# A Perceiver block with two mixtures of experts on one core: the first experts' matmuls with the rows as fixed side and the weights moving in two parts, and the second experts' weights chosen on GpSimd

## What is computed

```
# first experts: each row goes to 2 of 8 experts, F = 512, D = 256; no limit of rows per expert
probs = softmax(flat @ Wg); topp, topi = top_k(probs, 2); topp = topp / (sum(topp) + 1e-08)
for e in range(8):
    h = silu(flat @ W1[e]) * (flat @ W3[e])
    out = out + cw[:, e:e + 1] * (h @ W2[e])
# second experts: 2 of 8, F = 1024, each expert takes at most cap = 512 rows, in order
h = gelu(xg @ W1[e] + b1[e]); out = h @ W2[e] + b2[e]
final = zeros.at[buf].add(out * w)
```

## Time and profile before

| | us |
|---|---|
| median of 3 runs | 1272.7 (1271.81 to 1279.18) |
| profiled execution | 1282.01, its span 1280.2 |
| PE busy | 1119.4, 87% of the span |
| POOL busy | 785.9, 61% |
| DVE busy | 737.9, 58% |
| ACT busy | 603.9, 47% |

### The profile page before, as it was taken

One profiled execution on the slowest core, in us unless ns is written; L12 is line 12 of the kernel. 1 busy time (PEld: TensorE's weight loads), 2 busy tenths in 40 slices (PEclk: granted clock), 3 DMA queues, 4 the chain that ended last, 5 costly groups with the idle time before them and its releaser, 6 DMA issues. The chain is left out here.

```text
span 1280.2 us, 28023 instructions
## 1 busy us (share of the span) xinstructions
PE 1119.4 (87%) x8612; PEld 1031.6 (81%) x8613; DVE 737.9 (58%) x2263; ACT 603.9 (47%) x1404; POOL 785.9 (61%) x815
## 2 busy tenths in 40 slices
PE   4799999999999998898899639999998357998888
PEld 2599999999999997687677429999997236888777
DVE  5566666667666664755565572333332666666663
ACT  1556555565555652433767533444443432444331
POOL 0487778777777784144787505666664056667753
PEclk9899999999999997899999869999999667999989
DMA  3221111212111120692000422232322574543400
GB/s 110 75 69 56 50 53 49 70 51 68 53 49 53 54 77 4 152 364 76 1 0 0 65 77 38 46 49 49 49 45 37 167 211 107 148 116 89 103 5 9
DMA packets 72144, 94.24 MB, mean 74 GB/s; under 512 B 14828, under 2 KB 52160, under 8 KB 72096
## 3 DMA queue, kind: packets, MB, share of 16 engines
q1 hardware_dynamic: 53584, 73.00, 18.0%
q0 software_dynamic: 16032, 20.62, 9.9%
q10 hardware_dynamic: 2480, 0.03, 0.1%
HBM read 73.69 MB, written 22.18 MB: 75 GB/s over the span
## 5 line engine op out<-in xcount | busy, mean ns | idle before, releaser
L428 PE MATMUL xa_ob<-xa_v,xa_pT 128*128 128x65 f32 x1024 | 135.1, 276 | 0.2 <-DVE xa_pT L653 0.2
L495 POOL TENSOR_TENSOR xa_qbd<-qs,xw_c_mask8s 128x512 fp32r<-128x512 f32 x128 | 131.8, 1051 | 2.3 <-ACT xa_pr L583 2.2
L2450 PE MATMUL e_yb<-e_w2s,e_hTs 128*128 128x256 f32 x768 | 106.4, 305 | 29.5 <-DVE e_y L2599 20.5
L1862 POOL DMA_INDIRECT e_x<-rows,source x71 | 71.4, 1006 | 94.0 <-DMA rows<-weight 40.7
L2450 PEld LDWEIGHTS e_yb<-e_w2s,e_hTs 128*128 128x128 f32 x768 | 103.4, 214 | 31.4 <-DVE e_y L2599 21.7
L428 PEld LDWEIGHTS xa_ob<-xa_v,xa_pT 128*128 128x128 f32 x1024 | 126.5, 194 | 0.3 <-DVE xa_pT L653 0.3
L583 ACT ACTIVATE xa_pr<-xa_pr,xa_nm 128x257 f32<-128x257 f32 x256 | 109.6, 500 | 34.2 <-DVE xa_nm L649 34.2
L566 ACT ACTIVATE xa_kT<-xa_kvp,xw_bk 128x258 fp32r<-128x258 f32 x128 | 61.1, 477 | 131.6 <-PE xa_kvp L382 124.0
L642 DVE TENSOR_SCALAR_CACHE_REDUCE xa_pr<-xa_sc 128x257 f32<-128x257 f32 x256 | 98.0, 421 | 23.5 <-PE xa_sc L408 23.5
L1867 POOL DMA_INDIRECT base<-e_y,place x39 | 63.7, 1634 | 60.2 <-DVE e_y L2058 53.3
L525 POOL TENSOR_TENSOR xa_ol<-xa_om,xa_tl 128x256 f32<-128x256 f32 x64 | 47.0, 735 | 82.5 <-DVE xa_rinv L670 82.2
(11 more groups left out here) (343 smaller groups left out, 3251.6 us busy)
## 6 DMA issues: line engine op xcount, KB each, us to landing
e_w<-in_F_W SPq DMA_DIRECT2D x16, 1024.0 KB
w<-in_W SPq DMA_DIRECT2D x24, 512.0 KB, 9.5
xa_ctx<-in_ctxT SPq DMA_DIRECT2D x32, 257.0 KB, 3.0
xa_ctx<-in_ctxT SPq DMA_DIRECT2D x64, 128.5 KB, 3.1
xa_vb<-vlx SPq DMA_DIRECT2D x64, 128.0 KB
xs<-in_x SPq DMA_DIRECT2D x4, 512.0 KB, 4.1
base<-xs SPq DMA_DIRECT2D x4, 512.0 KB, 3.2
base<-xb POOLq DMA_DIRECT2D x4, 512.0 KB, 9.7
```

The source lines that it names most:

```text
L428: mm = pe.matmul(ob[:, 65 * g:65 * g + 65], pT[:, par, g, t, :], v[:, vs, t, g, :], start=(g == 0 and t == 0), stop=(g == G - 1 and t == 1 ...
L495: pool.tensor_tensor(dst, src, msk, ALU.mult).then_inc(q_ready, 1)
L1862: return pool.indirect_dma_start(out=out, out_offset=None, in_=rows, in_offset=bass.IndirectOffsetOnAxis(ap=index, axis=0))
L2450: mm = pe.matmul(yb[:, s % 2, 0:D], hTs[:, a, f, P * s:P * s + P], w2s[:, par, b, f, :], start=(f == 0 and (a, b) == (0, 0)), stop=(f == M ...
```

## The change

**First experts.** The rows become the fixed side, and the weights move. Rows, weights and hidden numbers are split into high part and rest and multiplied in float32r in three products: `hidden` is 6 matmuls of 512 columns, and its result has rows as partitions, so that the product h is turned by four transposes (`hb`), split by ScalarE and VectorE into `hTs`, and multiplied with `w2s` in 12 matmuls of 256 columns, which now come last in the step. The high parts of W1 and W3 of all experts are made once (`w1h`, `w3h`), the rests (`w13l`) in the place of the weights themselves. They are made by ScalarE and VectorE in the first routing, at the start of the phase and, by the tables `HIGH`, `REST1` and `REST3`, in the first steps; W2 is split anew for each tile (`high_w2`, `rest_w2`). The constant `steps` makes every expert own at least one tile, so that tile j never belongs to an expert above j. The first 8 steps are written out. The buffers `xs` and `oT`, and `nT` and `xb`, become two pairs whose memory then holds the high parts, hence the names xs_oT and nT_xb in the lists below.

**Second experts.** `choose_weights` moves from VectorE to GpSimd, ahead of the rests of each next expert. The rests of expert 0's weights move from GpSimd to the head of VectorE's list. ScalarE loads gelu's table in the routing, and scales expert 0's bias after its gelus.

```diff
-            np.tile(P * np.arange(T), (P, 1)), np.tile(np.arange(J1), (P, 1)), np.tile(p, (P, 1)),
+            np.tile(P * np.arange(T) - (np.arange(T) == 0), (P, 1)), np.tile(np.arange(J1), (P, 1)), np.tile(p, (P, 1)),
...
-            if not capped:
-                scalar_work(act)
+                early_work(act)
             act.wait_ge(tile_ready, 1)
             act.activation(values[:, :, 0, :], in_tile[:], ACT.Copy, scale=p1[:, 0:1]).then_inc(v0_ready, 1)
-            if capped:
-                scalar_work(act)
+            scalar_work(act)
...
+    at = {name: m.nc.alloc_sbuf_tensor_at("e1_" + name, [P, n * E, F1], F32R, offset=offset)
+          for (name, n), offset in zip((("w1h", 2), ("w3h", 2), ("w13l", 4)), places)}
...
+def high_w1_of(act, b, e):
+    act.activation(b["w1h"][:, 2 * e:2 * e + 2, :], b["w13"][:, 4 * e:4 * e + 2, :], ACT.Copy).then_inc(b["w1h_ready"], 1)
...
+def rest_w3_of(dve, b, e):
+    dve.wait_ge(b["w3h_ready"], e + 1)
+    dve.tensor_tensor(b["w13l"][:, 4 * e + 2:4 * e + 4, :], b["w13"][:, 4 * e + 2:4 * e + 4, :], b["w3h"][:, 2 * e:2 * e + 2, :],
+                      ALU.subtract).then_inc(b["w3l_ready"], 1)
+
+
+EARLY = 3
+HIGH = {0: (6,), 1: (7,)}
+REST1 = {0: (3,), 1: (4,), 2: (5,), 3: (6,), 4: (7,)}
+REST3 = {0: (2, 3), 1: (4,), 2: (5,), 3: (6,), 5: (7,)}
...
+            def hidden(bank, par, high, low, at):
+
+                for k in range(2):
+                    for a, part in PARTS:
+                        w = high[:, bass.ds(at[0] + k, 1), :] if part == 0 else low[:, bass.ds(at[1] + k, 1), :]
+                        mm = pe.matmul(bank[:], xTs[:, par, a, k, :], w.rearrange("p a f -> p (a f)"),
+                                       start=(k == 0 and (a, part) == (0, 0)), stop=(k == 1 and part == 1))
                 return mm
...
-                    pe.wait_ge(xT_ready, j * 2 + 2)
-                    pe.wait_ge(w1_ready, j + 1)
+                    e = pe.value_load(te[0:1, bass.ds(j, 1)], min_val=0, max_val=E - 1)
+                    pe.wait_ge(xl_ready, j + 1)
                     pe.wait_ge(s_ready, j)
-                    hidden(ab, par, 0).then_inc(a_ready, 1)
+                    if static(j) and j < E:
+                        pe.wait_ge(w1l_ready, j + 1)
+                    hidden(ab, par, w1h, w13l, (e * 2, e * 4)).then_inc(a_ready, 1)
                 if there(j, 1):
-                    d = pe.value_load(te[0:1, bass.ds(j - 1, 1)], min_val=0, max_val=E - 1)
                     pe.wait_ge(h_ready, j)
-                    pe.wait_ge(y_ready, j - 1)
+                    pe.wait_ge(hl_ready, j - 1)
                     for f in range(4):
-                        mm = pe.matmul(yb[:], hT[:, f, :], w2[:, bass.ds(d * 4 + f, 1), :].rearrange("p a c -> p (a c)"),
-                                       start=(f == 0), stop=(f == 3))
-                    mm.then_inc(yb_ready, 1)
+                        mm = pe.transpose(hb[:, f, :], h[:, P * f:P * f + P], ident[:])
+                    mm.then_inc(ht_ready, 1)
...
-                    pe.wait_ge(w3_ready, j + 1)
                     pe.wait_ge(h_ready, j)
-                    hidden(bb, par, 1).then_inc(b_ready, 1)
+                    if static(j) and j < E:
+                        pe.wait_ge(w3l_ready, j + 1)
+                    hidden(bb, par, w3h, w13l, (e * 2, e * 4 + 2)).then_inc(b_ready, 1)
+                if there(j, 1):
+                    pe.wait_ge(hh_ready, j)
+                    pe.wait_ge(hl_ready, j)
+                    pe.wait_ge(y_ready, j - 1)
+                    pe.wait_ge(w2l_ready, j)
+                    for f in range(4):
+                        for a, part in PARTS:
+                            mm = pe.matmul(yb[:], hTs[:, a, f, :], w2s[:, 1 - par, part, f, :],
+                                           start=(f == 0 and (a, part) == (0, 0)), stop=(f == 3 and part == 1))
+                    mm.then_inc(yb_ready, 1)
...
+                act.wait_ge(xl_ready, j)
+                for k in range(2):
...
+                act.activation(xTs[:, par, 0], xT[:], ACT.Copy).then_inc(xh_ready, 1)
...
+            def high_w2(j, par):
...
+                act.activation(w2s[:, par, 0], w2[:, bass.ds(e * 4, 4), :], ACT.Copy).then_inc(w2h_ready, 1)
...
+                if there(j, 1):
+                    act.wait_ge(ht_ready, j)
+                    act.wait_ge(yb_ready, j - 1)
+                    act.activation(hTs[:, 0], hb[:], ACT.Copy).then_inc(hh_ready, 1)
+                if there(j, -1):
+                    turn_x(j + 1, 1 - par)
...
+                    high_w2(j, par)
+                if static(j):
+                    for e in HIGH.get(j, ()):
+                        high_w1_of(act, b, e)
+                        high_w3_of(act, b, e)
+
+            high_w1_of(act, b, 3)
+            high_w3_of(act, b, 3)
             turn_x(0, 0)
-            tiles(act, step)
+            for e in (4, 5):
+                high_w1_of(act, b, e)
+                high_w3_of(act, b, e)
+            tiles(act, step, 1)
...
-                dve.tensor_copy(wd[:, par, 1], w13[:, bass.ds(e * 4 + 2, 2), :]).then_inc(w3_ready, 1)
+                dve.wait_ge(w2h_ready, j + 1)
+                dve.tensor_tensor(w2s[:, par, 1], w2[:, bass.ds(e * 4, 4), :], w2s[:, par, 0], ALU.subtract).then_inc(w2l_ready, 1)
...
+                    dve.wait_ge(b_ready, j + 1)
+                    if not static(j) or j >= 1:
+                        dve.wait_ge(ht_ready, j)
+                    dve.tensor_tensor(h[:], bb[:], s[:], ALU.mult).then_inc(h_ready, 1)
+                if static(j):
+                    for e in REST1.get(j, ()):
+                        rest_w1(e)
...
-                    if not isinstance(j, int) or j >= 3:
+                    dve.wait_ge(share_loaded[1 - par], ((j - 1) // 2 + 1) * 16 if static(j) else j * 8 + (0 if par == 0 else 8))
+                    if not static(j) or j >= 3:
                         dve.wait_ge(y_added, j * 16 - 32)
                     dve.scalar_tensor_tensor(out=y[:, 1 - par, :], in0=yb[:], scalar=share[:, bass.ds(j - 1, 1)], in1=ls2[:],
                                              op0=ALU.mult, op1=ALU.mult).then_inc(y_ready, 1)
-                if there(j, -1):
-                    copy_w3(j + 1, 1 - par)
                 if there(j, 0):
...
+                    rest_w2(j, par)
+                if static(j):
+                    for e in REST3.get(j, ()):
+                        rest_w3_of(dve, b, e)
+
+            rest_w1(0)
+            rest_w3_of(dve, b, 0)
+            rest_x(0, 0)
+            rest_w1(1)
             finish_shares()
+            rest_w3_of(dve, b, 1)
+            rest_w1(2)
             tiles(dve, step, 1)
...
+                if static(e) and e == 0:
+                    scale_b2(0, 0)
...
-            scale_b2(0, 0)
...
+            def choose_weights(e, par):
+                if e == 0:
...
+                for c in range(2):
+                    pool.tensor_tensor(wt[:, c, :], x[:, par, :, D + c], first[:, c, e * ST:e * ST + ST], ALU.mult).then_inc(wt_ready, 1)
+                pool.wait_ge(wt_ready, e * 2 + 2)
+                pool.tensor_tensor(ws[:, par, :], wt[:, 0, :], wt[:, 1, :], ALU.add).then_inc(ws_ready, 1)
...
                 if e + 1 < E:
+                    choose_weights(e + 1, 1 - par)
                     rest_w1(e + 1, 1 - par)
                     rest_w2(e + 1, 1 - par)
 
-            rest_w1(0, 0)
             gather(1, 1)
-            rest_w2(0, 0)
+            choose_weights(0, 0)
...
-                choose_weights(0, 0)
...
-                    choose_weights(e + 1, 1 - par)
...
+            for k in range(2):
+                dve.wait_ge(w1h_ready, k + 1)
+                dve.tensor_tensor(w1s[:, 1, k, :], w1[:, 0, k, :], w1s[:, 0, k, :], ALU.subtract).then_inc(w1l_ready, 1)
+            for c in range(2):
+                m = slice(M // 2 * c, M // 2 * c + M // 2)
+                dve.wait_ge(w2h_ready, c + 1)
+                dve.tensor_tensor(w2s[:, 0, 1, m, :], w2[:, 0, m, :], w2s[:, 0, 0, m, :], ALU.subtract).then_inc(w2l_ready, 1)
             split_first()
```

151 lines of the change are left out of this document (84 added, 67 removed).

## The result

The changed kernel takes 1225.7 us (median of 4 runs, 1225.03 to 1227.12); before took 1272.4 beside it. The ratio is 0.9622 (0.9593 to 0.9651), 46.6 us less. The forecast was 57.2 us less and 1216, with a range of 1203 to 1240. The profiled executions, 1282.01 and 1225.03, differ by 57.0. Timed again, the changed kernel took 50.6 us less than before (1223.9 and 1274.5 beside it).

What follows compares the result with a forecast made beforehand. PE was taken to bound the first experts, and VectorE's small operations held behind GpSimd's subtractions to delay the second. Terms of -13.5 and -43.7 gave -57.2 off the median 1272.7: 1215.5, forecast 1216, range 1203 to 1240.

Steps and rivals of the forecast that it cites:

- Both readings: First experts: PE's own work sets the time; second experts: VectorE's small operations wait behind GpSimd's subtractions, 5 us per expert.
- The term for experts 1 to 7: Second experts after expert 0: -34.1 us without the wait, +2.4 for GpSimd being late.
- this execution is 9.3 above the median, so I take the difference off the median: Whole kernel: subtract the 57.2 us gain from the median 1272.7, not from the profiled 1282.0, giving 1215.5.
- -13.5: First experts, head and steady steps together: us gained, with bounds from +5 to -17.
- The head: Start of the first experts: first output 5.6 us later, then 29.7 us for five steps held by VectorE's subtractions.
- 33 x 4.9: First experts, steady steps: 33 steps at 4.9 us each, PE's matmuls and turns plus a handoff, instead of 5.57.
- I charge nothing: First experts: GpSimd's add starts before VectorE's rest of W2, so their shared port costs 0 us.
- Rival (a): First experts gain nothing: adds land no closer than 5.5 us, or rests delay issues; term about +3, 1232 us; chance 0.19.
- rival (c): First experts: VectorE's SBUF-only operations wait out GpSimd issues, tiles some 7.3 us, kernel slower at 1296 us; chance 0.04.
- Tightest hop: First experts: turned product, ScalarE's copy, VectorE's rest, output matmuls take 1.6 us, matched by 1.6 of other PE work.
- Its rests leave GpSimd, so nothing blocks VectorE's casts: Second experts, expert 0: VectorE's casts run freely during `e_hb`, so it takes 25.6 us instead of 38.6, -13.0.
- Rival (b): Second experts: GpSimd becomes the bound, choosing costs 3.6 us, round 25.9, 20 us lost, 1236 us; chance 0.12.

Runs made afterwards that it cites:

- the second profile: The kernel before, unchanged, profiled once more: 1275.35 us, against 1282.01 for its first profiled execution.
- the two second profiles: Repeat profiles of the unchanged kernel before (1275.35 us) and of the unchanged changed kernel (median of its timed runs 1223.9 us).

## Why the prediction was right, and where its steps were off

**The bounds.** Both readings held. PE bounded the first experts and does so still; the second experts' 5 us per round were VectorE's small operations behind GpSimd's subtractions. The choosing alone is worth 33 us by the ratios, 34 by the times (1260.0 - 1225.7). The term for experts 1 to 7 was -31.7, measured -33.9. The move took away 3 us of waiting per round and with it the stretch at a lower clock behind each wait.

**Median and profiled execution.** The step that cost most was the last: "this execution is 9.3 above the median, so I take the difference off the median". The terms were sized on an execution whose excess lay largely in the waits that the change removes (4.4 of the 6.7 us by which the second profile is shorter); the kernel after has none, and its runs lie within 2.1 and 4.1 us of each other (before's first runs within 7.4). Taken from the profiled execution, the forecast was 1224.8 for 1225.03. The terms should have been sized with rounds of a usual execution, or the sum set against 1282.0 alone.

**Luck.** That -57.2 met -57.0 is luck: the first experts gave 4.7 us less than forecast, the second experts 2.9 more, and 1.6 came from stages that the change leaves alone. Sized on before's second profile (1275.35), the second experts' terms would have come out 4.4 us smaller.

**First experts.** The sign was right, the size was not: first gather to last add -8.8 where -13.5 stood, and -10 by the two second profiles (225.0 and 215.1). The head was less bad than feared (+3.5 for +5.6; the first five steps 27.1 us for 29.7). The term "33 x 4.9" was 170.6 us: PE's own step is 4.96 and 5.13, since groups take up to 0.1 us more where they change than matmuls counted at 0.229 and 0.114 (1.50 for the 12 output matmuls, not 1.37); late in the loop the tiles took 5.34 for eight steps; and the stall at its end cost some 3 us in this execution. The sum also ended with the last output matmul, at 974.6 for 976.8 measured. But the path goes on through the last adds, each waiting up to 3.0 us for the one before to land: the last add started 2.7 us behind the last output, and 1.2 in before.

**The port.** "I charge nothing" was right for the quiet tiles and wrong for the late ones. What the runs show: an issue that starts inside VectorE's subtraction ends 1.50 us (add) or 0.85 us (gather) after that subtraction's end; one that has started is left alone. The forecast's "half a microsecond" was one case of it. The first seven adds paid it too, behind the head's subtractions. From 920 us on it could keep itself up, a stretched add making the next one late, to the loop's end in one profile and to 941 us in the other. The Trainium skill, "SBUF — State Buffer", section "SBUF: two separate sides", says that while VectorE runs an operation in a two-port mode (its example is a float32 copy) GpSimd can't write the descriptors of its DMAs. The traces show the same for a subtraction, where an issue starts inside it (2.50 us at 952.37), and not for an issue under way (1.62 us at 869.97). The forecast's reading of it, "each issue met by a rest of W2 would last 1.2 us longer", was too wide.

Rival (a), with its adds no closer than 5.5 us, and rival (c) did not happen. That "no row of the loop shows two of them closer than 5.5" was misread: the trace of before has adds 5.33 us apart in the loop, and 4.75 and 4.61 apart behind it. And by the forecast's own sum, tiles of 5.5 us give +6.3 for the term, not +3 or +5.

**"Tightest hop".** The forecast checked a hop of 1.6 us and the engines' busy sums, and missed the ring of 4.87 us. It happened to fit under PE's step, by a quarter of a microsecond in one tile and by nothing in the next; that too was luck.

**Expert 0.** The term was right in size (-14.2 for -13.0, of which 1.1 is only that the first 48 matmuls took 12.59 us and not 13.73), its reason was wrong. "Its rests leave GpSimd, so nothing blocks VectorE's casts" named an edit that is worth nothing in the time: 1.8 us gained behind `e_hb`, 1.7 given back in the first gathers, which start inside VectorE's rests now (1.99 and 1.97 us instead of 0.95). With the rests and the choosing each on its old or new engine, expert 0 took:

| | choosing on VectorE | choosing on GpSimd |
|---|---|---|
| rests of expert 0 on GpSimd | 38.4, 37.4 | 26.3 |
| rests on VectorE | 29.5 | 24.2, 25.1 |

Either edit alone takes away the second collision, in which the last splits met the next expert's subtractions. With the rests on VectorE no cast is held, and the last split ends 15.7 us behind `e_hb`, before GpSimd starts its subtractions (17.1; choosing on VectorE). With the choosing on GpSimd ahead of them, and with `scale_b2` behind the gelus, GpSimd starts 17.6 us behind `e_hb` and not 15.1. The run with the choosing behind the rests of W1 brings one caught split back, and 3.7 us of the 11 to 12; it supports this, and the rest is argued. The share of `scale_b2` wasn't tried.

**Rival (b)** stayed away, but narrowly: three small operations cost 0.56 us, where I took 1.8 with the port, and the +2.4 for it came out as nothing. GpSimd's rounds are still longer than PE's, and of its reserve 0.87 us were left at expert 6. Its price was near: 2.4 us more per round cost 15 us, which is its kind of sum (rounds too long by 2.9 us, less 5 of reserve) without the 6 that it added for collisions.
